# Attention gate and mixture of experts on one core: the scales of W1 and W2 in two steps, W split from chunk 3 on, W2's sums in six parts, h of tile 0 ahead of group 1's maxima

## What is computed

```python
# attention: only the sums of the exponentials are used
q, k = rope(bf16(x @ Wq.T)), rope(bf16(x @ Wk.T))
o = where(causal, exp(q @ k.T / 16), 0).sum(-1)
x1 = layernorm(x + relu(o * fc1_w + fc1_b) @ fc2_w.T + fc2_b)
# mixture: three routings of the same address, top 3 of 12, softmax over the three
xa = x1 @ P_w.T
C1, C2, C3 = (combine(xa @ U.T) for U in (U1, U2, U3))
h = gelu(sum_e C1[:, e] * (x1 @ W1[e].T))
y = sum_e C2[:, e] * (h @ W2[e].T) + C3 @ b2
out = layernorm(x1 + y)
```

## Time and profile before

| | us |
|---|---|
| median of three runs | 300.6 (300.32 to 302.5) |
| the profiled execution's own time | 304.48 |
| its span, first to last instruction | 302.5 |
| busy: PE, DVE, ACT, POOL | 271.4, 248.2, 164.1, 144.3 |
| mean granted clock of PE | 0.966 of 2.4 GHz |

### The profile page before, as it was taken

How to read it: one execution, slowest core, us unless ns; L and a number is a source line. 1 busy time by engine, 2 the same in 40 slices (tenths; PEclk the granted TensorE clock), 3 DMA queues, 4 the chain that set the end, 5 groups by cost and what they waited for, 6 DMA issues and landing times.

```text
span 302.5 us, 6418 instructions
## 1 busy us (share of the span) xinstructions
PE 271.4 (90%) x2028; PEld 196.4 (65%) x2030; DVE 248.2 (82%) x728; ACT 164.1 (54%) x341; POOL 144.3 (48%) x315
## 2 busy tenths in 40 slices
PE   7997999997959974999999999999999999999980
PEld 5443444553526663797877877777778878788960
DVE  0368498999966985879999999999999989987872
ACT  1246745765736446036746846837846946545430
POOL 0200006999998752432482383374364362474421
PEclk9999899999979995799999999999999999999997
DMA  8997999970000000001001001000100101010111
GB/s 234 419 386 265 165 190 202 144 101 0 0 1 2 1 2 0 0 2 37 20 20 36 20 18 32 23 20 21 31 25 18 37 20 36 20 35 22 36 35 39
DMA packets 19211, 20.50 MB, mean 68 GB/s; under 512 B 1620, under 2 KB 18408, under 8 KB 18664
## 3 DMA queue, kind: packets, MB, share of 16 engines
q1 hardware_dynamic: 18456, 19.13, 26.7%
q10 hardware_dynamic: 720, 0.93, 1.0%
HBM read 15.83 MB, written 4.19 MB: 66 GB/s over the span
## 4 chain that ended last, share of the span: by engine, by line
PE 57%; DVE 24%; issue 7%; SPq 4%; DMA 4%; ACT 2%; POOL 0%; DVEq 0%; POOLq 0%
PE bank L935 37%; PE bank L773 8%; DVE early L1303 7%; DMA W<-in_w2T 4%; PE bank L821 4%; SPq L338 2%; DVE early L1360 2%; DVE xsin L1079 2%; PE bank L786 2%; DVE top L1172 2%; DVE zrest L1187 2%; PE bank L832 2%; DVE st L1355 1%; DVE x1T L1162 1%; DVE xcos L1078 1%
## 5 line engine op out<-in xcount | busy, mean ns | idle before, releaser
L935 PE MATMUL bank<-W,early 128*128 (+1 forms) x630 | 75.7, 276 | 5.3 <-DVE early L1360 5.3
L935 PE MATMUL bank<-W,x1T 128*128 (+1 forms) x630 | 74.9, 273 | 0.6 <-DVE early L1303 0.3
L935 PEld LDWEIGHTS bank<-W,early 128*128 128x128 f16 x630 | 60.3, 99 | 17.1 <-DVE early L1360 7.0
L935 PEld LDWEIGHTS bank<-W,x1T 128*128 128x128 f16 x630 | 59.8, 98 | 11.3 <-issue 2.5
L1303 DVE SCALAR_TENSOR_TENSOR early<-bank,Csel,early 128x256 f32<-128x256 f32 x124 | 59.7, 482 | 8.1 <-PE bank L935 3.7
L773 PE MATMUL bank<-early,wqk 128*128 128x512 f32 x128 | 63.2, 627 | 2.8 <-ACT qk L561 1.9
L773 PEld LDWEIGHTS bank<-early,wqk 128*128 128x128 f32 x128 | 23.2, 197 | 24.3 <-issue 21.8
L682 ACT ACTIVATE early<-early 128x256 f32<-128x256 f32 x32 | 13.3, 417 | 45.1 <-DVE early L1303 44.9
L561 ACT ACTIVATE qk<-bank 128x512 bf16<-128x512 f32 x32 | 18.9, 594 | 34.3 <-PE bank L773 34.2
L519 POOL TENSOR_SCALAR ve<-mv 128x1 f32<-128x1 f32 x32 | 7.3, 227 | 60.5 <-DVE mv L1356 59.9
L1078 DVE TENSOR_TENSOR xcos<-qk,cb 128x1024 bf16<-128x1024 bf16 x16 | 11.9, 746 | 20.3 <-ACT qk L561 20.2
(11 more groups left out here) (117 smaller groups left out, 453.6 us busy)
## 6 DMA issues: line engine op xcount, KB each, us to landing
early<-in_xT SPq DMA_DIRECT2D x16, 256.0 KB, 7.2
xs<-in_x SPq DMA_DIRECT2D x32, 128.0 KB, 7.8
out<-early SPq DMA_DIRECT2D x32, 128.0 KB
W<-in_w1T SPq DMA_DIRECT2D x1, 2048.0 KB, 11.8
W<-in_w2T SPq DMA_DIRECT2D x1, 2048.0 KB, 12.5
W<-in_w1T SPq DMA_DIRECT2D x1, 1024.0 KB, 7.1
W<-in_w2T SPq DMA_DIRECT2D x1, 1024.0 KB, 14.1
wqk<-in_wqkT ACTq DMA_DIRECT2D x1, 512.0 KB, 3.7
```

The lines of the kernel that those rows point to most:

```text
L935: mm = pe.matmul(where[:, 0:DIM], lhs(hx, c), w, start=(k == 0), stop=(k == 5))
```

## The change

1. ACT sums |W2| in six parts of two matrices, three in chunk 2 and three in chunk 3, none in chunk 1.
2. The scales come in two steps. Step 0 is the router and W1: `peak_transpose(0)` at the end of PE's chunk 2, `peak_pow(0)` at the end of DVE's, `peak_spread(0)` behind `project(3, 0)`, `scales(0)` in DVE's chunk 3 ahead of `rope(3, 0)`. Step 1 is W2: `w_bound` ahead of `router_split` in chunk 4, `peak_transpose(1)` behind `project(4, 1)`, `peak_pow(1)` ahead of `rope(4, 1)`, `peak_spread(1)` behind `project(4, 3)`, `scales(1)` ahead of `rope(5, 0)`.
3. POOL's pieces run from chunk 3 to chunk 6 (three in chunk 3, the last two behind one another). What needs W2's scale waits for step 1. ACT and DVE split two matrices in each of chunks 3, 4 and 5 and two among the experts.
4. Transpose and split of h of tile 0 leave loop i: PE has the transpose behind the first mixture of tile 1 and ahead of `aux(0,0,1)`; ACT has `begin(1)`, `gelu(0)`, `normed(2,0)`, high part, `gelu(1)`, then `exp_route(1)`; DVE has the sums of tile 1, the low part, then `aux(0,0,0)`.

```diff
+        HIGH = {3: (0, 1), 4: (2, 3), 5: (4, 5)}
+        HALVES = [slice(p.start + 2 * n, p.start + 2 * n + 2) for p in PARTS for n in range(2)]
+        STEPS = (slice(0, 2), slice(2, 3))
 # POOL
-                if n == 0:
-                    pool.wait_ge(scale_done, 1)
+                if n % (NE - NB) == 0:
+                    pool.wait_ge(scale_done, m + 1)
...
                     early_aux(c, j, early)
-                    if c >= 4:
+                    if (c, j) != (3, 3) and 3 <= c < NCH - 1:
                         w_piece(piece)
                         piece += 1
+                    if (c, j) == (NCH - 2, 3):
+                        w_piece(piece)
+            C3_split(0)
+            select_of(0)
             norm_scale(2)
-            w_piece(piece)
 # ACT
-                act.activation(junk[:, :, :], Wf[:, WS:2 * WS, :][:, PARTS[q], :], ACT.Abs,
+                wait(act, asum_done, q - 1)
+                r = q % 2
+                act.activation(junk[:, 2 * r:2 * r + 2, :], Wf[:, WS:2 * WS, :][:, HALVES[q], :], ACT.Abs,
                                accum_out=amaxp[:, 1, q:q + 1]).then_inc(asum_done, 1)
-                if q < 2:
-                    act.wait_ge(asum_done, q + 1)
...
-                act.wait_ge(scale_done, 1)
+                act.wait_ge(scale_done, m + 1)
...
                 early_aux(c, 1, early)
-                if c == 2:
-                    w_sum(1)
-                if c in (4, 5):
-                    w_high(2 * (c - 4))
+                if c in (2, 3):
+                    w_sum(3 * (c - 2))
+                if c in HIGH:
+                    w_high(HIGH[c][0])
                 qk_copy(c, 2)
                 if c:
                     exps(c - 1, 1)
+                if c in (2, 3):
+                    w_sum(3 * (c - 2) + 1)
                 qk_copy(c, 3)
...
-                if c in (1, 2):
-                    w_sum(2 * (c - 1))
-                if c in (4, 5):
-                    w_high(2 * (c - 4) + 1)
+                if c in (2, 3):
+                    w_sum(3 * (c - 2) + 2)
+                if c in HIGH:
+                    w_high(HIGH[c][1])
...
             begin(1)
-            w_high(NB + 3)
+            gelu(0)
             normed(2, 0)
+            h_high(0)
+            gelu(1)
             aux(0, 0, 0)
-            gelu(0)
             aux(0, 0, 1)
 # PE
                 project(c, 0)
+                if c == 3:
+                    peak_spread(0)
                 early_aux(c, 0, early)
                 project(c, 1)
+                if c == 4:
+                    peak_transpose(1)
...
                 project(c, 3)
-                if c == 3:
-                    peak_spread()
+                if c == 2:
+                    peak_transpose(0)
+                if c == 4:
+                    peak_spread(1)
                 early_aux(c, 3, early)
...
             mixture(1, 0, lambda hx, c: x1T[:, 1, hx, c, :], range(TOPK))
+            pe.wait_ge(hgT_copied, NCH)
+            h_transpose(0)
             aux(0, 0, 1)
 # DVE
                 early_aux(c, 1, early)
+                if c == 3:
+                    scales(0)
                 if c == 4:
-                    scales()
+                    w_bound()
                     router_split()
+                if c == 5:
+                    scales(1)
                 rope(c, 0)
...
+                if c == 2:
+                    w_amax(2)
                 early_aux(c, 2, early)
-                if c in (4, 5):
-                    w_low(2 * (c - 4))
+                if c in HIGH:
+                    w_low(HIGH[c][0])
                 early_aux(c, 3, early)
...
+                if c == 4:
+                    peak_pow(1)
                 rope(c, 1)
...
                 if c == 2:
-                    w_amax(2)
-                    w_bound()
-                if c in (4, 5):
-                    w_low(2 * (c - 4) + 1)
+                    peak_pow(0)
+                if c in HIGH:
+                    w_low(HIGH[c][1])
...
             w_low(NB + 3)
+            first_mixture(1)
+            h_low(0)
             aux(0, 0, 0)
-            first_mixture(1)
             aux(0, 0, 1)
```

More of the change, by code:

```diff
@@ L682, in gelu, with h_high @@
                 act.activation(hact[:, t % 2, :], acc1[:, t % 2, :], ACT.Gelu).then_inc(gelu_done, 1)
+            def h_high(t):
+                act.wait_ge(hT_done, t + 1)
+                act.activation(hT[:, t % 2, 0, :, :].rearrange("p c n -> p (c n)"), bank[HT][:, 0:DIM], ACT.Copy,
+                               scale=ipow2[:, 1:2]).then_inc(hhi_done, 1)
             for c in range(NCH):
@@ L728, in _ @@
                 aux(k, s, 0)
-                if i <= NT:
-                    t = i - 1
-                    act.wait_ge(hT_done, t + 1)
-                    act.activation(hT[:, t % 2, 0, :, :].rearrange("p c n -> p (c n)"), bank[HT][:, 0:DIM], ACT.Copy,
-                                   scale=ipow2[:, 1:2]).then_inc(hhi_done, 1)
+                if 1 < i <= NT:
+                    h_high(i - 1)
                 aux(k, s, 1)
@@ L797, in gate_transpose, with peak_transpose, peak_spread @@
                 tr.then_inc(hgT_done, 1)
-            def peak_transpose():
-                pe.wait_ge(amax_done, 3)
-                pe.transpose(bank[MISC][0:3, 0:P], amax[:, :], identf[:, :]).then_inc(peak_done, 1)
-            def peak_spread():
-                pe.wait_ge(diag_done, 1)
-                pe.matmul(bank[MISC][:, P:P + 3], ones3[:, :], diag[:, :], start=True, stop=True).then_inc(bcast_done, 1)
+            def peak_transpose(n):
+                cols = STEPS[n]
+                pe.wait_ge(amax_done, cols.stop)
+                wait(pe, scale_done, n)
+                pe.transpose(bank[MISC][0:cols.stop - cols.start, 0:P], amax[:, cols], identf[:, :]).then_inc(peak_done, 1)
+            def peak_spread(n):
+                cols = STEPS[n]
+                rows = slice(0, cols.stop - cols.start)
+                pe.wait_ge(diag_done, n + 1)
+                pe.matmul(bank[MISC][:, P + cols.start:P + cols.stop], ones3[rows, :], diag[rows, cols],
+                          start=True, stop=True).then_inc(bcast_done, 1)
             begun = {"fc": 0, "bias": 0, "x1T": 0, "C3T": 0, "logits": 0, "count": 0}
@@ L953, in load_ids, with h_transpose @@
                 held_ids[g] = v
+            def h_transpose(t):
+                pe.wait_ge(gelu_done, t + 1)
+                wait(pe, hlo_done, t)
+                for c in range(NC):
+                    tr = pe.transpose(bank[HT][:, c * P:(c + 1) * P], hact[:, t % 2, c * P:(c + 1) * P], identf[:, :])
+                tr.then_inc(hT_done, 1)
             pe.wait_ge(zero_done, 1)
@@ L1023, in _ @@
                     mixture(t, 1, lambda hx, c: hT[:, t % 2, hx, c, :], range(experts_of(t)))
-                if i <= NT:
-                    t = i - 1
-                    pe.wait_ge(gelu_done, t + 1)
-                    wait(pe, hlo_done, t)
-                    for c in range(NC):
-                        tr = pe.transpose(bank[HT][:, c * P:(c + 1) * P], hact[:, t % 2, c * P:(c + 1) * P], identf[:, :])
-                    tr.then_inc(hT_done, 1)
+                if 1 < i <= NT:
+                    h_transpose(i - 1)
                 aux(k, s, 1)
@@ new lines, in scales @@
+            def scales(n):
+                cols = STEPS[n]
+                dve.wait_ge(bcast_done, n + 1)
+                link(dve.tensor_copy(pow2[:, cols], bank[MISC][:, P + cols.start:P + cols.stop]))
+                dve.reciprocal(ipow2[:, cols], pow2[:, cols])
+                link(dve.tensor_scalar(iscale[:, cols], pow2[:, cols], 1.0 / TOP, None, ALU.mult))
+                if n == 0:
+                    dve.memset(cscale[:, 2:3], 1.0)
+                    dve.tensor_copy(cscale[:, 0:1], iscale[:, 1:2])
+                else:
+                    link(dve.tensor_tensor(cscale[:, 1:2], iscale[:, 2:3], pow2[:, 1:2], ALU.mult))
+                dve.tensor_scalar(scale[:, cols], ipow2[:, cols], TOP, None, ALU.mult).then_inc(scale_done, 1)
```

74 lines of the change are left out of this document (26 added, 48 removed).

## The result

The changed kernel takes 307.75 us (median of four runs, 306.88 to 308.42) against 301.36 for the kernel before in the same comparison: ratio 1.021, 95% interval 1.0156 to 1.0263. The prediction was 307.5, and the median came out as forecast. Between the two profiled executions, though, the time rose from 304.48 to 308.42, by 3.9 us and not by the 7.0 of the sum.

What follows compares the result with a forecast made beforehand. DVE was taken to bound chunks 4 to 6 and PE the experts of tile 0. 5.0 us (chunks) plus 2.0 (h first) made 7.0 on the 300.6 median, called 307.5; range 299.5 to 311, the forecast's own 304 to 310.

Steps and rivals of the forecast that it cites:

- W2's sums: Chunks 2 and 3: earlier W2 sums let rope(3,0) start at 39.7 in place of 40.65, minus 0.95 us.
- Split from chunk 3: From rope(3,0) to rope(4,0): plus 2.2 us, rope(4,0) 1.25 later at 52.75; before 51.5 would show it wrong.
- Second step of the scales: Chunk 4: PE waits for w_bound and peak_pow(1), x1_low not before 67.1 (plus 4.2), chunk 5's rope 5.0 us late.
- the 5.0 stays: From rope(5,0) to the first expert product: same DVE instructions, pieces beside them in both kernels, so 5.0 us remains.
- Rival (3): Ropes beside POOL's pieces: half the hindrance, decided by a mean rope of 3.0 us down; minus 7.5, 300; chance 0.14.
- End of the split: POOL's pieces up to chosen_exps: 6 to 7 us later, at 96 to 97; cost taken as 0, bounds 0 and plus 2.
- they return nothing: Experts of tile 0: PE bounds that stage, so taking two w_high and two w_low out returns nothing.
- h first: "plus 2.0": Behind begin(1): group 1's maxima and bias(0,0) wait longer for h, plus 2.0 us, bounds 0 and 2.5.
- Rival (1): The low clock comes after both new PE waits, at 33 and 59: plus 3.3, 311 us; chance 0.15.
- rival (2): PE's hand-overs in time: DVE's waits at fc(0,0) 1.4, rope(3,0) 1.0, x1_low 2.1 covered; minus 4.5, 303; chance 0.17.
- Rival (4): A table change ahead of gelu(0) costs ACT twice its load, another 1.28 us: 308.9; chance 0.04.
- rival (5): W2 lands after 28, ACT waits as before, up to 2 us: 307 to 309; chance 0.50 together with the forecast.

## Why the prediction was right, and where it was not

- *W2's sums: "minus 0.95".* PE's wait of 1.7 at the first transpose and ACT without a wait came as written. In the profiles rope(3,0) moves by minus 1.32. But the kernel before had a stretch at the low clock there in its profiled execution; where it had none (the run with w_low earlier, same code up to there) rope(3,0) starts at 39.03, so against that the change gains nothing. One new thing holds DVE: rows of x land only for 37.75. It isn't what ends last, as rope(3,0) waits another 0.29 us for its copies.
- *Split from chunk 3: rope(4,0) "at 52.75".* It came at 51.15, and the "wrong" sign at 51.5 is met. From rope(3,0) to rope(4,0) it is 11.82 us for 10.85, plus 1.0 rather than plus 2.2; router_split took 0.66 rather than 1.5.
- *Second step of the scales: x1_low "not before 67.1", rope(5,0) "5.0 late".* 65.34 and 67.42. Against 63.47, less the 1.62 us of low clock at 30 to 34 that rope(3,0) shows (40.65 for 39.03), rope(5,0) is 5.6 late: right in size. Of PE's two waits in chunk 4 the first is there (2.29), and so is that of x1_low (2.50). **The second, at 56 for peak_pow(1), is not.** The projection behind the first wait ran at 1.2 GHz and took 3.19 us (1.94 at the full clock), so PE reached peak_spread(1) only at 57.16, when peak_pow(1) was done. In the kernel with h at its old place the clock stayed at 1.00 from 50 to 55, and there PE waits:

```profile
56.93 0.38 PE L815 MATMUL bank<-diag,ones 1*128 1x1 f32 x2 [1.35 <-DVE diag L1128]
```

Either way peak_spread(1) starts at about 57, and rope(5,0) at 67.42 and 67.18. The low clock and the wait stand in each other's place here and don't add up.

- *"From there to the first expert product ... the 5.0 stays."* **This step failed.** From rope(5,0) to the product it is 27.80 us for 31.53 in the profiles, so 3.7 of the 3.95 are given back. One part is the ropes (lengths from the start of the first operation to the end of the last, us):

| rope | before: start, length | changed: start, length |
|---|---|---|
| (5,0) | 63.47, 3.73 | 67.42, 2.78 |
| (5,1) | 71.16, 3.05 | 74.71, 2.08 |
| (6,0) | 76.77, 3.82 | 79.68, 3.74 |
| (6,1) | 82.44, 4.18 | 85.26, 3.27 |

The four take 11.87 us for 14.78, two w_low 0.85 more: minus 2.05. The second operation of rope(5,1), before and in the changed kernel:

```profile
71.76 1.65 DVE L1079 TENSOR_TENSOR xsin<-qk,cb 128x1024 bf16<-128x1024 bf16 x1
75.31 0.68 DVE L1098 TENSOR_TENSOR xsin<-qk,cb 128x1024 bf16<-128x1024 bf16 x1
```

The first ran beside a piece that POOL began at 71.36, the second beside POOL's norm_scale, which began at 74.32. "The same instructions, with pieces beside them in both" fixed neither what stood beside a rope nor its length. The other part, 1.7 us, is chance: the low clock behind PE's wait at scores(6,0). From the end of rope(6,1) to the product it is 8.38 us in the profiled execution of before, 6.68 in that kernel with h first, where the clock didn't fall there, and 6.69 in the changed kernel, where the wait is 0.31 for 3.10. Against an execution of before without its two slow stretches the first product is thus 0.22 + 1.62 + 1.7 = 3.5 us late (an estimate from these rows): of 5.6 us, 3.5 stay. Rival (3) named the ropes, with a mean of 3.0 as its point, and "ropes beside pieces under 3 us" was a "wrong" sign; the six ropes of the changed kernel average 2.9 (17.44 of six). Its time of 300 didn't come, since from the logits on PE has 20.4 us of work of its own, and the run with few pieces shows that shorter ropes buy no earlier product.

- *End of the split: "0, bounds 0 and plus 2".* chosen_exps at 94.72, a wait of 3.39 at esum and of 1.05 at scores(7,0); 1.0 us by the run that moves the pieces. Inside the bounds.
- *"Two w_high and two w_low leave the experts ... they return nothing."* **This step failed too.** PE is full in that stage, but DVE isn't done when PE is: the maxima queue behind the last w_low. Without h first, the stage behind mixture(1) gets 3.9 us shorter (12.50 to 8.64).
- *h first: "plus 2.0".* Right for the kernel before (1.84 in the stage, 2.4 by time), and right as a chain; bias(0,0) comes 7.26 us behind begin(1) as said. In the changed kernel it costs 5.7, as it sets the maxima 4.90 us behind mixture(1), and by then they could have started with it.

That the total came out is luck in two places. At the experts a gain of 3.9 us that was not seen and a loss of 5.7 that was put at 2.0 leave plus 1.85 in the profiles, as if only h had been there. And the spans of the two profiles differ by 3.9 us, not 7.0: 0.22 + 0.96 + 1.85 + 0.9 for the four columns of the table. But the profiled execution of before had both of its stretches at the low clock (below), while the 300.6 on which the 7.0 was put is a median of three, two of which (300.32 and 300.6) took what executions without either stretch take, 300.2 to 300.7. Against such an execution the estimate is 3.5 + 0.96 + 1.85 + 0.9 = 7.2: 1.5 less in the chunks than said, and 1.0 for POOL's late pieces and 0.9 behind mixture(0,1), which the sum had at 0. No run explains the 0.9; in the other runs it is 180.2 to 181.2 us from there to the end, in the changed kernel 181.3. Against the median of the 81 later runs of the kernel before, 302.8, the changed kernel is 4.9 us slower.

Rival (1) had the low clock at the waits at 33 and 59. It came behind neither, but behind the second transpose (0.68 from 50 to 55) and behind the logits (0.83 from 72 to 82). Of rival (2), one hand-over was in time: rope(3,0) waited 0.29 us for its copies, not 1.0. Rival (4) is out by the rows of the table load above, rival (5) as well, as ACT had W2 in time.

## What to carry to other kernels

Where one engine is full, work taken from another can still pay: here DVE finished its queue after the full PE did, and the next stage waited for what stood behind that queue. So look at what comes next in the queue of the engine that gives up work, and count the gain there. A move that costs 2 us can cost 6 once another edit has made room at the same place, so edits that meet at one wait have to be tried apart. Before a delay is carried forward through "the same instructions", ask which engine is the bound at the far end. And take a difference and the base that it is added to from executions at the same clock.
